# Adding one key block of the attention probabilities onto another by DMA, with two more probability buffers

## The reference

```
xn = layernorm(layernorm(x), g1);  q = xn @ Wq.T;  k, v = split(xn @ Wkv.T)
q, k = l2norm(16 * q) * 4, l2norm(k) * 4
sim = einsum('bhid,bjd->bhij', q, k);  sim = where(causal_mask, max_neg, sim)
attn = softmax(sim);  out = einsum('bhij,bjd->bhid', attn, v)
out = layernorm(out @ Wout.T, g2)
h = silu(xn0 @ wg.T) * (xn0 @ wu.T);  x = x + out + h @ wd.T
```

## Time and profile before

| | |
|---|---|
| median of 3 runs | 1293.28 us |
| the profiled execution, its own time | 1296.09 us |
| its span | 1294.2 us |
| PE busy | 1170.9 us, 90% of the span |
| DVE, ACT, POOL busy | 68%, 52%, 35% |
| layer 2, eight sequences | from about 655 us to the end |

### The profile page before, as it was taken

One profiled execution on the slowest core, in us unless ns is written; L12 is line 12 of the kernel. 1 busy time (PEld: TensorE's weight loads), 2 busy tenths in 40 slices (PEclk: granted clock), 3 DMA queues, 4 the chain that ended last, 5 costly groups with the idle time before them and its releaser, 6 DMA issues. The chain is left out here.

```text
span 1294.2 us, 26914 instructions
## 1 busy us (share of the span) xinstructions
PE 1170.9 (90%) x8812; PEld 799.3 (62%) x8812; DVE 883.1 (68%) x2412; ACT 672.5 (52%) x1294; POOL 457.9 (35%) x687
## 2 busy tenths in 40 slices
PE   5999999999999995799399899998999989999896
PEld 3556566566666653689365766657666676766664
DVE  6888888888888865455355766657666576665744
ACT  2666666666667661355164452644527355263540
POOL 4222212222221225543343361634615345253440
PEclk9999999999999996799699999999999999999999
DMA  2310001000000005222000000000000000000000
GB/s 63 103 25 17 18 18 25 17 17 18 20 23 17 17 10 188 65 61 55 15 10 1 9 8 0 16 0 8 8 0 16 0 10 6 0 16 0 9 1 9
DMA packets 34597, 29.78 MB, mean 23 GB/s; under 512 B 5984, under 2 KB 27104, under 8 KB 34528
## 3 DMA queue, kind: packets, MB, share of 16 engines
q1 hardware_dynamic: 32224, 24.22, 6.7%
q0 software_dynamic: 2304, 4.72, 1.6%
HBM read 13.72 MB, written 6.82 MB: 16 GB/s over the span
## 5 line engine op out<-in xcount | busy, mean ns | idle before, releaser
L1295 ACT ACTIVATE arena<-ring_a 128x384 f32<-128x384 f32 (+1 forms) x512 | 252.6, 550 | 139.8 <-PE ring_a L477 139.8
L1440 ACT ACTIVATE arena<-ring_a 128x1024 f32<-128x1024 f32 x128 | 131.7, 1029 | 156.9 <-PE ring_a L477 156.9
L1058 POOL TENSOR_SCALAR_AFFINE_SELECT arena<-arena 128x512 f32<-128x512 f32 x128 | 81.9, 640 | 356.2 <-ACT arena L1295 356.2
L477 PE MATMUL ring_a<-q_max,rows 128*128 128x384 f32 (+1 forms) x512 | 195.4, 385 | 1.1 <-ACT arena L1295 0.5
L1580 DVE CUSTOM_DVE_ANT_0 arena<-pair,arena 128x384 bf16<-128x384 f32 (+1 forms) x271 | 162.3, 614 | 25.8 <-PE pair L477 22.7
L1202 POOL TENSOR_TENSOR q_len<-q_sum,exponents 128x8 f32<-128x8 f32 x64 | 108.2, 1690 | 141.8 <-DVE q_sum L1869 141.8
L477 PE MATMUL pair<-arena,v_aug 128*64 128x512 f32 (+3 forms) x1024 | 150.2, 438 | 4.0 <-ACT arena L1440 3.5
L477 PE MATMUL ring_a<-rows,k_rows 64*128 64x384 f32 (+2 forms) x1152 | 125.1, 339 | 14.8 <-DVE rows L1888 13.8
L477 PE MATMUL ring_a<-arena,v_aug 128*32 128x384 f32 (+1 forms) x1024 | 122.8, 551 | 2.1 <-POOL arena L1058 1.0
L477 PEld LDWEIGHTS pair<-arena,v_aug 128*64 128x64 f32 x1024 | 68.4, 136 | 85.4 <-issue 68.0
L1230 POOL TENSOR_SCALAR_AFFINE_SELECT arena<-arena 128x256 f32<-128x256 f32 x256 | 96.1, 406 | 56.0 <-ACT arena L1440 56.0
(11 more groups left out here) (255 smaller groups left out, 2199.6 us busy)
## 6 DMA issues: line engine op xcount, KB each, us to landing
rows<-k_rows SPq DMA_DIRECT2D x128, 64.0 KB, 2.0
arena<-in_w SPq DMA_DIRECT2D x2, 2048.0 KB, 14.1
slots_y<-arena SPq DMA_DIRECT2D x40, 64.0 KB
x_all<-in_x SPq DMA_DIRECT2D x8, 256.0 KB, 3.5
tokens_x<-xn_all SPq DMA_DIRECT2D x1, 2048.0 KB, 9.5
out<-o_t SPq DMA_DIRECT2D x8, 256.0 KB, 2.3
arena<-tokens_x,tokens_now POOLq DMA_INDIRECT x40, 2.5
wq_sb<-in_wq_t SPq DMA_DIRECT2D x1, 512.0 KB, 4.8
```

Of the source, the lines that this page charges most:

```text
L477: return pe.matmul(out, lhs, rhs, start=start, stop=stop, skip_group_check=True)
L1058: pool.affine_select(out=v, in_=v, compare_op=ALU.is_ge, fill=0.0, base=0, pattern=[[0, HG], [1 if late else -1, P]], channel_multiplier=- ...
L1295: act.activation(probs[:, t % NT, h, 0:many], A.slot(("cols", c))[:, 0:many], ACT.Exp).then_inc(A.free.sem, A.free.add(1))
L1440: act.activation(dst, src, ACT.Exp).then_inc(ring.free.sem, ring.free.add(1))
```

## The change

Four things are changed in layer 2, and where two tiles of layer 1 lie in memory.

- For pairs 0 to 5 (`N_FOLD = 6`) POOL issues a DMA that adds block 1's probabilities (2 heads by 384 columns on 128 partitions, f32, 393,216 bytes) onto columns 128 to 511 of block 0's (`fold(n)`). It stands in POOL's step n + 2, behind `q_length` and ahead of the masks. It waits for `o_full` of pair n, so that `values1(n)` has read the probabilities as they were, and, from the second on, until the fold before it has landed.
- `sums1(m)` for m = 0, 1, 2 waits until both its folds have landed, and then sums blocks 0, 2 and 3 only: 24 instructions where there were 32.
- `sums1(0), (1), (2)` stand in steps 4, 6 and 7 (before: 2, 4, 6). `sums1(3)` stays where it was and sums four blocks.
- There are six probability buffers (before: four). The two new ones and the split queries lie in memory that layer 1's `sel` and `rows` used; ACT waits for the first `sums1` before pairs 6 and 7 only.

```diff
--- before.py
+++ after.py
@@ -60,7 +60,8 @@
 PAD = TT // 2
 H1, D1 = 16, 64
 NP = H1 // 2
-QB, PB = 3, 4
+QB, PB = 3, 6
+N_FOLD = 6
 QSCALE1, NORM_EPS, ROOT_SCALE = 16.0, 1e-12, 4.0
 HID = 384
 HC = HID // P
@@ -94,7 +95,8 @@
              picked=1, back=16 * NT, added=1)
 PER_C = dict(squared=6, q_full=6, q_free=6, o_full=7, o_free=7, l_full=1, l_free=1, s_full=15, s_free=15, m_full=8, m_free=8, w_full=11, w_free=11,
              e_full=10, e_free=9, own=18, var=1, veps=1, rstd=1,
-             sums=6, lens=6, q_lo=8, h1=3, masked=24, pv=4, g_free=2, inverted=1, fin=1, stored=16)
+             sums=6, lens=6, q_lo=8, h1=3, masked=24, pv=4, g_free=2, inverted=1, fin=1, stored=16,
+             folded=16 * N_FOLD)
 
 CREDITED = dict(q_lo=1, q_free=1, o_free=1, l_free=1, s_free=1, m_free=1, w_free=1, e_free=1, g_free=1, sums=1, h1=1, r_free=1, added=1, stored=1, pv=1,
                 xt_free=1, y_full=1, y_free=1, staged=2, out0=1, out1=1, out2=1, out3=1)
@@ -284,7 +286,6 @@
         ident = sb("ident", [P, P])
         ones_row, sumlo_neg = (sb(n, [P, 1]) for n in ("ones_row", "sumlo_neg"))
         rows2 = sb("rows2", [P, 2, HG])
-        sel = sb("sel", [P, G, 4, HG, 4, D0], F32R)
         rev_e = sb("rev_e", [P, NT, NE])
         pick_sum = sb("pick_sum", [P, HG, 32])
         spread = sb("spread", [P, NP, P], F32R)
@@ -307,7 +308,6 @@
         full, hi = fulls[:, 0, :], halves[:, 0, :]
         k_rows, q_rows = sb("k_rows", [P, 2, T], F32R), sb("q_rows", [P, 2, T], F32R)
         q_max = sb("q_max", [P, 2, T], F32R)
-        rows = sb("rows", [P, H0, T], F32R)
         v_aug = sb("v_aug", [P, NT, H0, 32])
         mx = sb("mx", [P, 2, HG, NT])
         m_cols = sb("m_cols", [P, NT, HG, 32])
@@ -322,6 +322,10 @@
         k_stack = k_rows
         q_sum, q_len, q_rn = sb("q_sum", [P, H1]), sb("q_len", [P, H1]), sb("q_rn", [P, H1])
 
+        with nc.sbuf_tensor("sel", [P, G, 4, HG, 4, D0], F32R) as sel, nc.sbuf_tensor("rows", [P, H0, T], F32R) as rows:
+            pass
+        q_parts = sb("q_parts", [P, 2 * QB, T], F32R)
+        late = sb("late", [P, 2, 2560])
 
         probs = arena[:, 0:NT * HG * T].rearrange("p (q h t) -> p q h t", q=NT, h=HG)
         at = NT * HG * T
@@ -347,7 +351,12 @@
         parts = spare[:, 0:2 * TT * NS].rearrange("p (t a s) -> p t a s", t=TT, a=2)
         tile_steps, tile_rows = parts[:, :, 0, :], parts[:, :, 1, :]
 
-        probs1 = arena[:, 0:10240].rearrange("p (n t) -> p n t", n=PB)
+        probs1 = [arena[:, n * 2560:n * 2560 + 2560] for n in range(4)] + [late[:, n] for n in range(2)]
+
+        def probs_of(n, j):
+
+            at, many, step, skip = ((1536, 512, 512, 0), (512, 384, 512, 0), (0, 256, 256, 0), (512, 128, 512, 384))[j]
+            return probs1[n % PB][:, at:at + 2 * step].rearrange("p (c t) -> p c t", c=2)[:, :, skip:skip + many]
         o1 = arena[:, 10240:14336].rearrange("p (n t) -> p n t", n=NP)
         x_hi, x_lo = q_rows[:, 0, :], q_rows[:, 1, :]
         q_sq = arena[:, 14336:14848].rearrange("p (g d) -> p g d", d=D1)
@@ -355,7 +364,7 @@
         q_nat = [t.rearrange("p (g d) -> p g d", d=D1) for t in
                  (q_nat_sb[:], o_n[:].rearrange("p i e -> p (i e)"))]
         k_nat = k_nat_sb[:].rearrange("p (i r d) -> p i r d", i=NT, r=2)
-        q_hi, q_lo = rows[:, 0:QB, :], rows[:, QB:2 * QB, :]
+        q_hi, q_lo = q_parts[:, 0:QB, :], q_parts[:, QB:2 * QB, :]
         kf, kn = (arena[:, at:at + 256].rearrange("p (i d) -> p i d", i=NT) for at in (15360, 15616))
         y_back = arena[:, 15872:16384].rearrange("p (i e) -> p i e", i=NT)
         spare = xn_all[:].rearrange("p t e -> p (t e)")
@@ -805,7 +814,7 @@
                 def p_of(n, c, j):
                     at, many = ((1536, 512), (512, 384), (0, 256), (896, 128))[j]
                     at += c * (256 if j == 2 else 512)
-                    return probs1[:, n % PB, at:at + many]
+                    return probs1[n % PB][:, at:at + many]
 
                 def values1(n):
                     pe.wait_ge(s["masked"].sem, s["masked"].at(b, 3 * (n + 1)))
@@ -820,7 +829,9 @@
 
                     if m == 0:
                         pe.wait_ge(s["g_free"].sem, s["g_free"].at(b, 0))
-                    for j in range(NT):
+                    if m < N_FOLD // 2:
+                        pe.wait_ge(s["folded"].sem, s["folded"].at(b, 32 * (m + 1)))
+                    for j in (0, 2, 3) if m < N_FOLD // 2 else range(NT):
                         for h in range(HG):
                             ins = mm(gather[32 * h:32 * h + 32, j * P:T], pick_sum[:, m, :], p_of(2 * m + h // 2, h % 2, j),
                                      start=(m == 0 and j == 0), stop=(m == NP // 2 - 1 and j == NT - 1))
@@ -841,8 +852,8 @@
                         gate_up(n + 1)
                     if n:
                         values1(n - 1)
-                        if n % 2 == 0:
-                            sums1(n // 2 - 1)
+                        if n in (4, 6, 7):
+                            sums1((4, 6, 7).index(n))
                 values1(NP - 1)
                 if not last:
                     turn_x(b + 1)
@@ -1214,10 +1225,22 @@
                 for name in () if last else ("veps", "rstd", "lens"):
                     SR[name].restart()
 
+                def fold(n):
+
+                    pool.wait_ge(s["o_full"].sem, s["O"].filled(b, ("o", n)))
+                    if n:
+                        pool.wait_ge(s["folded"].sem, s["folded"].at(b, 16 * n))
+                    apart(pool)
+                    pool.dma_start(probs_of(n, 0)[:, :, P:T], probs_of(n, 1),
+                                   accum_op=ALU.add).then_inc(s["folded"].sem, s["folded"].add(16))
+
+                s["folded"].restart()
                 for n in range(NP):
                     if n + 2 < NP:
                         q_length(s, n + 1, b)
-                    p = probs1[:, n % PB]
+                    if 0 <= n - 2 < N_FOLD:
+                        fold(n - 2)
+                    p = probs1[n % PB]
                     for third, ring in enumerate((s["M"], s["S"], s["W"])):
                         pool.wait_ge(ring.free.sem, ring.emptied(b, ("probs", n, third)))
                         apart(pool)
@@ -1432,8 +1455,8 @@
                     at, many = ((512, 1024), (0, 512), (1536, 1024))[third]
                     act.wait_ge(ring.full.sem, ring.filled(b, ("probs", n, third)))
                     if third == 0:
-                        act.wait_ge(s["pv"].sem, s["pv"].at(b, max(n // 2 - 1, 0)))
-                    dst, src = probs1[:, n % PB, at:at + many], ring.slot(("probs", n, third))[:]
+                        act.wait_ge(s["pv"].sem, s["pv"].at(b, 1 if n >= PB else 0))
+                    dst, src = probs1[n % PB][:, at:at + many], ring.slot(("probs", n, third))[:]
                     if third == 1:
                         dst, src = (v.rearrange("p (c t) -> p c t", c=2) for v in (dst, pair[:]))
                         src = src[:, :, 0:256]
```

## The result

The changed kernel takes 1336.57 us (median of 4 runs, 1335.41 to 1337.63) where the kernel before takes 1293.44 in the same comparison: ratio 1.0331, 95% interval 1.0314 to 1.0349, 43 us slower. The forecast had the direction (1310, range 1283 to 1370) and 16.6 of the 43 us.

What follows compares the result with a forecast made beforehand. PE, busy 90% of the span, was taken to bound the kernel, with other engines barely in time in short steps. Savings of 16.6 us against stands and late masks gave +16.6 us net, about 1310 us, range 1283 to 1370.

Steps and rivals of the forecast that it cites:

- What goes: PE's `sums1(0)` to `sums1(2)` without block 1: 0.69 us less each, 2.07 a sequence, 16.6 in all; group 58.5 us busy.
- What is moved: Three `sums1` go from steps 2, 4, 6 to 4, 6, 7, with six buffers: gains nothing, memory places cost nothing.
- POOL's time for a fold: POOL's own time to issue one accumulating DMA: 1.25 us plus 0.15 idle, 1.40.
- The stand before `project_q(6)`: In step 4 PE waits about 1.8 us, as a fold delays `q_length` for pair 6; seven sequences, not the last.
- Masks late: A fold puts POOL's masks back by 1.4 us against about the same slack; 0.2 us a sequence in step 5.
- Landing of a fold: From a fold's issue on POOL to its semaphore: 4.7 us (1.25 + 0.6 + 2.6 + 0.25).
- Three in a row: Folds 3 to 5, each waiting for the one before, have 11.75 us; PE stands 2.35 us before `sums1(2)`.
- The sum: +2.3 us in each of seven sequences with a fetch, +0.5 in the last: +16.6 us, median about 1310.
- Rival 1: Folds land in time, 3.9 us or less, so no stand before `sums1(2)`: 1291 or 1284 us; chance 0.40.
- Rival 2: The accumulate is far slower than a copy, landing in 7.3 us: 1372 us; chance 0.12.
- rival 3: POOL's issue is the price, 2.5 us a fold, with more lost in step 4 and at masks: 1330 us; chance 0.08.

Runs made afterwards that it cites:

- e1_order: Changed kernel without folds: six buffers and the new places of the sums, all four blocks summed; 1295.12 us, ratio 1.0004 to the kernel before.
- e3_own: Changed kernel with one semaphore per fold, so POOL no longer waits for the fold before; 1304.36 us, ratio 1.0070 to the kernel before.
- e9_copy: As e2_issue, but the DMA is a plain copy of the same 384 KB without the addition; 1304.7 us in a single run.
- e12_ahead_again: The kernel of e10_ahead timed again on another chip; 1281.70 us against 1293.40 for the kernel before, ratio 0.9908.
- e2_issue: Changed kernel with folds added onto an unused tile, PE summing all four blocks and waiting for no fold; 1319.47 us, ratio 1.0184 to the kernel before.
- e7_busy: Changed kernel plus three unused 512-column matmuls in step 7 before the wait of `sums1(2)`; 1337.43 us, ratio 1.0293 to the kernel before.
- e10_ahead: Changed kernel with own semaphores, later sums, no fold in step 2, fold 1 ahead of step 4's masks; 1296.71 us, ratio 0.9972 to the kernel before.

## Why the prediction was right or wrong

The terms of the sum came out close to what they measured. What failed is the sum itself (point 7): it had no term for the lower clock behind a stand, and none for what a fold does to the instructions beside it.

1. *What goes* (2.07 us a sequence, 16.6): right where the clock is 1.00. The sums take 1.64 us (854.48 to 856.12) for 2.29, so 0.65 each and 15.6 us in all; the prediction had 0.69. The group's 58.5 us busy, "the step that I am surest of", measured 66.6: the six slow `sums1(2)` hold 6.5 of the 8.1 us between.
2. *What is moved* costs nothing: right (e1_order, 1.0004).
3. *POOL's time for a fold* (1.25 us): right, 1.28 for the folds 0 to 3, 1.20 for the two in the late buffers. What it does to the instructions beside it was not in the prediction: masks of 1.48 us take 1.9 to 3.1, and L1850 0.67 us for 0.25, which puts 0.33 us before `project_q(5)` in step 3, 2.9 us of step length in all.
4. *The stand before `project_q(6)`* (1.8 us in seven sequences, 12.6): right, 13.0 us in 7 times, and none in the eighth. It was 2.04 in five and 1.4 in two.
5. *Masks late* (0.2 us a sequence in step 5, 1.6): right in size by luck. There are four waits, 2.1 us in all, in steps 4 and 6 of the first and the seventh sequence (0.41 and 0.66 us; 0.40 and 0.67), and none in step 5.
6. *Landing of a fold* (4.7 us): right, 4.5. *Three in a row* (2.35 us before `sums1(2)`, 18.8): right, 20.8 us in 8. e3_own shows that it is the row and not the bytes.
7. *The sum* failed in a term that it did not have. Every stand was priced at its own length and the work behind it at the 2.4 GHz level: what the clock costs was put at nothing, without a reason. Behind nine of the fifteen stands the clock was granted at 0.50 for some 3 us, which cost 1.6 us each, 14.4 in all (step 4: 11.3 for 9.7; step 7: 36.1 for 34.5). The trace before has no such stand from scores to scores: the longest is 1.1 us, and PEclk was 1.00 over the 80 us that I looked at the earlier trace rows, which I took as a property of the stage and not of its having no gaps. To the 16.6 come 14.4 of the clock, 2.9 of step 3, 2.4 more in the stands, 1.0 less saved in the sums and 0.5 more for masks: 37.8. A tenth fall, behind the stand of 1.90 us at the end of the last sequence, adds 1.6: 39.4. No fold stands there, and eight of the fourteen profiles show this fall, with folds placed well or badly, so it can't be put down to the change. The profile's 39.2 is not thereby explained in full: the first scores of layer 2 begin 3.7 us earlier than in the kernel before (647.42 for 651.09), so layer 2 is 42.9 us longer, and 3.5 us of it were not placed.

Rival 1 needed a landing of 3.9 us or less: a copy has it (2.9), the accumulate hasn't (4.5). The rule of the Trainium skill, DMA: Bandwidth & Descriptors (section Anatomy of one DMA, SWDGE (gpsimd) path), gives an estimate of 2.9 us for these bytes, which is e9_copy's number and not the fold's. The Trainium skill's other rule, of Collectives: The Full Stack (section The bandwidth ceiling: the fold count and why AG ≠ RS ≠ AR), that a reduction by DMA has half the rate of a copy, agrees with the transfer, 2.3 us for 1.25.

Rival 2 (7.3 us to land) and rival 3 (2.5 us of POOL) are both out by the profile, though 1337 us lies nearest to rival 3's 1330: the time alone would have spoken for the wrong mechanism.

The cost is not in the idea. With the same folds in other places (e12_ahead_again) 11.7 of the 15.6 us show. The loss of 43 us is 59 us of cost less the gain of 15.6. Some 32 of the 59 were three dependent DMAs in 11.7 us (e3_own takes them away); most of the rest was one DMA on an engine that had nothing free in that step (e2_issue, 24 us). Each was made larger by the clock.

## What to carry to other kernels

Before a transfer takes work from the busiest engine, lay its issue, its landing and its dependents on the timeline of each step: n dependent DMAs need n landings, and an issue on GpSimd is an instruction of its queue like any other, paid by what stands behind it. Where TensorE has run without a gap, price a new gap of 2 us with up to 1.6 us on top, since the work behind it may run at half the clock (here it did behind 25 of 39 such gaps); and if a gap can't be closed, moving other work into it can be worth more than its length. A chain that is just in time in the profile may be 0.3 us late on another chip.

## What the runs showed of the hardware that was not expected

- Behind the first scores of layer 2, a stand of PE of 2.0 to 2.7 us was followed by a granted clock of 0.50 for about 3 us in nine of thirteen cases in the changed kernel, and not in the other four, with lengths that do not tell them apart (2.04 us both times). In the profiles of the changed kernel, e2_issue to e7_busy together, the stand of 2.0 us in step 4 was followed by it in 25 of 39 cases and the one of 1.4 us in none of ten. The stand of 1.90 us at the end of the last sequence, which every kernel has, was followed by it in eight of the fourteen profiles, among them the changed kernel and not the one before. The stands of 1.1 us and less in the kernel before and of 0.6 us in e9_copy were not followed by it. What decides between fall and no fall stays open.
- An accumulating DMA of 384 KB within SBUF lands 4.5 us after its issue, its bytes moving in 2.3 us, about 170 GB/s; the copy lands after 2.9 us, its bytes moving in 1.25 us, about 315 GB/s. It costs POOL 1.28 us against 0.79.
- A small instruction of DVE (128x8, 0.25 us) and POOL's own masks mostly take 0.4 us or more longer when a fold is issued on POOL beside them. The fold may not be all of it: in e10_ahead the same DVE instruction takes 1.33 us in step 4 of seven sequences (at 841.08 in the third), beside the masks, while the fold's row begins only at 842.34. In the timelines the masks' row begins before the fold's has ended, so POOL's durations there overlap.
